# Ring depths of four, four and three in a routed expert stage, with the result store issued by ScalarE

## The reference

```
x = x + 0.5 * experts(layernorm(x))        # 8 experts, top 2, hidden width 256
x = x + attention(layernorm(x))            # 16 heads of 8, softmax, per batch
x = x + 0.5 * experts(layernorm(x))        # the same weights again
x = x + 0.5 * fp4_ffn(layernorm(x))        # weights and activations rounded to FP4 in blocks of 16
x = x + retention(layernorm(x))            # 16 heads, decay, group norm
x = x + 0.5 * fp4_ffn(layernorm(x))
```

## Time and profile before

| | us |
|---|---|
| median of 2 runs (2268.72 and 2268.86) | 2268.79 |
| profiled execution, its own time | 2260.8 |
| its span, first to last instruction | 2259.0 |
| TensorE busy in the span (matmul) | 1542.7 (68%) |
| VectorE, ScalarE, GpSimd busy | 1171.3, 940.7, 557.6 |
| TensorE's mean granted clock | 0.815 of full |

### The profile page before, as it was taken

The page is one execution under the profiler, slowest core; times in us unless marked ns, Lnnn a source line. Parts: engine busy times, 40 slices in busy tenths (PEclk is TensorE's granted clock), DMA queues, the critical chain, the costliest instruction groups (busy, mean ns, idle before and its releaser), DMA issues.

```text
span 2259.0 us, 25733 instructions
## 1 busy us (share of the span) xinstructions
PE 1542.7 (68%) x9017; PEld 837.3 (37%) x9017; DVE 1171.3 (52%) x1765; ACT 940.7 (42%) x1957; POOL 557.6 (25%) x966
## 2 busy tenths in 40 slices
PE   4345454555559999999999853454545467899777
PEld 3234343443111111111111232343434345666566
DVE  5200001111959999999999352111011139968896
ACT  1111111112158888888888721111111134566464
POOL 5720022125440000000000247100222026444411
PEclk9866666777569999999999975666666677999898
DMA  5221222222110101101001022212222210000001
GB/s 188 89 77 58 70 75 81 71 82 91 56 61 18 32 21 32 32 18 44 21 23 32 8 73 89 79 59 70 73 80 70 70 49 19 1 2 2 2 1 38
DMA packets 97457, 116.23 MB, mean 51 GB/s; under 512 B 14368, under 2 KB 76512, under 8 KB 97104
## 3 DMA queue, kind: packets, MB, share of 16 engines
q1 hardware_dynamic: 89136, 97.78, 14.6%
q0 software_dynamic: 8192, 16.79, 2.4%
HBM read 82.28 MB, written 35.26 MB: 52 GB/s over the span
## 4 chain that ended last, share of the span: by engine, by line
PE 52%; DMA 12%; DVE 11%; issue 7%; POOL 6%; ACT 6%; SPq 5%; POOLq 0%; ACTq 0%; DVEq 0%
PE PS L569 13%; DMA slots_in<-slots_x 11%; PE PS L1030 11%; PE PS L1018 8%; PE PS L581 4%; PE PS L1007 4%; DVE neg_half L1165 3%; PE PS L558 3%; ACT probs L1106 2%; POOL slots_x L472 2%; SPq L512 2%; PE PS L1715 2%; SPq L514 2%; ACT slots_out L636 2%; SPq L531 1%
## 5 line engine op out<-in xcount | busy, mean ns | idle before, releaser
L1165 DVE TENSOR_REDUCE neg_half<-PS 128x2 f32<-128x1024 f32 x512 | 601.4, 1220 | 73.2 <-PE PS L1007 58.1
L1106 ACT ACTIVATE probs<-PS 128x512 f32<-128x512 f32 x1024 | 528.8, 603 | 110.8 <-PE PS L1018 109.8
L711 DVE TENSOR_TENSOR shared<-shared,PS 128x512 f32<-128x512 f32 x92 | 63.3, 688 | 830.8 <-PE PS L569 740.4
L558 PE MATMUL PS<-ident,slots_in 128*128 128x128 f32 x184 | 61.4, 436 | 466.9 <-DMA slots_in<-slots_x 444.4
L569 PE MATMUL PS<-slotsT,w_ring 128*128 128x256 f32 x736 | 322.2, 616 | 0.0
L1018 PE MATMUL PS<-qk_all 51*128 51x512 bf16 x1024 | 278.5, 386 | 23.6 <-ACT probs L1106 17.9
L1030 PE MATMUL PS<-probs,Vg 128*32 128x512 f32 x2048 | 273.6, 606 | 0.1
L569 PEld LDWEIGHTS PS<-slotsT,w_ring 128*128 128x128 f32 x736 | 228.9, 326 | 47.5
L623 ACT ACTIVATE slotsT<-PS 128x256 f32<-128x256 f32 x92 | 35.3, 384 | 495.3 <-PE PS L558 471.8
L487 POOL DMA_INDIRECT came<-slots_y,place x128 | 127.9, 999 | 460.6 <-DMA slots_y<-slots_out 423.1
L1007 PE MATMUL PS<-qk_all 48*128 48x512 bf16 x1024 | 199.4, 400 | 42.6 <-DVE neg_half L1165 25.5
(11 more groups left out here) (217 smaller groups left out, 1949.2 us busy)
## 6 DMA issues: line engine op xcount, KB each, us to landing
w_ring<-in_w_experts SPq DMA_DIRECT2D x92, 384.0 KB, 3.1
slots_in<-slots_x SPq DMA_DIRECT2D x92, 128.0 KB, 3.0
slots_y<-slots_out SPq DMA_DIRECT2D x92, 128.0 KB, 1.8
split<-qk_all SPq DMA_DIRECT2D x16, 384.0 KB, 3.3
qk_all<-split SPq DMA_DIRECT2D x64, 96.0 KB
qk_all<-split SPq DMA_DIRECT2D x64, 64.0 KB
slots_x<-tokens_all,place POOLq DMA_INDIRECT x128, 2.2
came<-slots_y,place POOLq DMA_INDIRECT x128, 2.6
```

Of the source, the lines that this page charges most:

```text
L558: last = pe.transpose(bank(0)[:, j * P:(j + 1) * P], slots_in[:, k % RING_TILES, j, :], ident[:, :])
L1106: act.activation(probs[:, n % 2, STRIPS * strip + pair, :], bank(RING_AT + use % RING), ACT.Exp, scale=ATT_SCALE).then_inc(s["exped"], 1)
L1165: dve.tensor_reduce(neg_half[m % 2][:, i % 2, :, at], bank(use_bank(i, m), 2).rearrange("p (s w) -> p s w", s=STRIPS), AX.X, ALU.max, nega ...
```

## The change

The single length `RING_TILES = 3` becomes three lengths: four places for weights, four for rows, three for results. The loads of SP run further ahead: weights three tiles, rows four tiles, and in a turn the rows come before the weights. The store of a tile's results leaves SP and goes to ScalarE's queue: in turn i ScalarE issues, after `result(i)`, the store of tile i - 1, and the last tile's store after the loop. The waits of the loads keep their meaning (a place must be free before it is filled), with the new lengths.

```
-RING_TILES = 3
+W_RING, IN_RING, OUT_RING = 4, 4, 3
...
         def moe_load_weights(sp, n, i):
             k = tile_of(n, i)
-            part, r = i // PART_TILES, k % RING_TILES
+            part, r = i // PART_TILES, k % W_RING
...
-            wait(sp, moe["y_ps"], k - RING_TILES + 1)
+            wait(sp, moe["y_ps"], k - W_RING + 1)
...
         def moe_load_slots(sp, n, i):
...
-            wait(sp, moe["in_ps"], k - RING_TILES + 1)
+            wait(sp, moe["in_ps"], k - IN_RING + 1)
...
-        def moe_store_slots(sp, n, i):
+        def moe_store_slots(act, n, i):
             k = tile_of(n, i)
-            part, r = i // PART_TILES, k % RING_TILES
-            sp.wait_ge(moe["y"], k + 1)
+            part, r = i // PART_TILES, k % OUT_RING
+            act.wait_ge(moe["y"], k + 1)
             at = i % PART_TILES * SLOTS_TILE
-            sp.dma_start(slots_y[part][at:at + SLOTS_TILE, :].rearrange("(j p) c -> p j c", p=P),
+            act.dma_start(slots_y[part][at:at + SLOTS_TILE, :].rearrange("(j p) c -> p j c", p=P),
...
         def moe_sp(sp, n, at_tile=None, between=None):
-            AHEAD = RING_TILES - 1
-            for i in range(AHEAD):
+            for i in range(W_RING - 1):
                 moe_load_weights(sp, n, i)
             if between is not None:
                 between()
-            for i in range(AHEAD):
+            for i in range(IN_RING):
                 moe_load_slots(sp, n, i)
             for i in range(STAGE_TILES):
-                if i + AHEAD < STAGE_TILES:
-                    moe_load_weights(sp, n, i + AHEAD)
-                    moe_load_slots(sp, n, i + AHEAD)
-                moe_store_slots(sp, n, i)
+                if i + IN_RING < STAGE_TILES:
+                    moe_load_slots(sp, n, i + IN_RING)
+                if i + W_RING - 1 < STAGE_TILES:
+                    moe_load_weights(sp, n, i + W_RING - 1)
...
             def result(i):
                 k = tile_of(n, i)
                 act.wait_ge(s["y_ps"], k + 1)
-                wait(act, s[f"out{k % RING_TILES}"], 16 * (k // RING_TILES))
+                wait(act, s[f"out{k % OUT_RING}"], 16 * (k // OUT_RING))
...
                 result(i)
+                if i > 0:
+                    moe_store_slots(act, n, i - 1)
                 if n == 0:
                     prep_act_at(act, i - PART_TILES)
+            moe_store_slots(act, n, STAGE_TILES - 1)
```

More of the change, by code:

```diff
@@ L106, in macaron @@
         rank = sb("rank", [P, TILES, EXPERTS])
-        w_ring = sb("w_ring", [P, RING_TILES, EXPERT_WORDS])
-        slots_in = sb("slots_in", [P, RING_TILES, SLOTS_TILE // P, C])
+        w_ring = sb("w_ring", [P, W_RING, EXPERT_WORDS])
+        slots_in = sb("slots_in", [P, IN_RING, SLOTS_TILE // P, C])
         slotsT = sb("slotsT", [P, 2, SLOTS_TILE])
-        slots_out = sb("slots_out", [P, RING_TILES, SLOTS_TILE])
+        slots_out = sb("slots_out", [P, OUT_RING, SLOTS_TILE])
         came = sb("came", [P, 2, GT, 2, C])
@@ L233, in macaron @@
         moe = stage_sems(ctx, nc, "moe", "xn xT_ps xT logit_ps logits shifted exped weighed members counts experts place scattered0 scattered1 "
-                         "w0 w1 w2 in0 in1 in2 out0 out1 out2 in_ps inT gu silu0 silu h y_ps y came0 came1 half_added x_acc")
+                         "w0 w1 w2 w3 in0 in1 in2 in3 out0 out1 out2 in_ps inT gu silu0 silu h y_ps y came0 came1 half_added x_acc")
         att = stage_sems(ctx, nc, "att", "xn xT_ps xTf q_ps k_ps qkf_half v_ps v_raw qkf rest1 part2 parts V to_dram0 to_dram1 strips filled read neg_step "
@@ L339, in uses_of @@
         def uses_of(k, slot):
-            return (k - slot + RING_TILES - 1) // RING_TILES
+            return (k - slot + OUT_RING - 1) // OUT_RING
         def moe_tokens(dve, n, g):
@@ L481, in moe_gather @@
                 end = tile_of(n, (part + 1) * PART_TILES)
-                for r in range(RING_TILES):
+                for r in range(OUT_RING):
                     pool.wait_ge(moe[f"out{r}"], 16 * uses_of(end, r))
@@ L517, in moe_load_slots @@
             k = tile_of(n, i)
-            part, r = i // PART_TILES, k % RING_TILES
+            part, r = i // PART_TILES, k % IN_RING
             if i % PART_TILES == 0:
                 sp.wait_ge(moe[f"scattered{part}"], SCATTERED * (n // 2 + 1))
-            wait(sp, moe["in_ps"], k - RING_TILES + 1)
+            wait(sp, moe["in_ps"], k - IN_RING + 1)
             at = i % PART_TILES * SLOTS_TILE
@@ L554, in turned @@
                 k = tile_of(n, i)
-                pe.wait_ge(s[f"in{k % RING_TILES}"], 16 * (k // RING_TILES + 1))
+                pe.wait_ge(s[f"in{k % IN_RING}"], 16 * (k // IN_RING + 1))
                 wait(pe, s["inT"], k)
                 for j in range(SLOTS_TILE // P):
-                    last = pe.transpose(bank(0)[:, j * P:(j + 1) * P], slots_in[:, k % RING_TILES, j, :], ident[:, :])
+                    last = pe.transpose(bank(0)[:, j * P:(j + 1) * P], slots_in[:, k % IN_RING, j, :], ident[:, :])
                 last.then_inc(s["in_ps"], 1)
@@ L562, in gate_up @@
                 k = tile_of(n, i)
-                w = w_ring[:, k % RING_TILES, :]
+                w = w_ring[:, k % W_RING, :]
                 pe.wait_ge(s["inT"], k + 1)
-                pe.wait_ge(s[f"w{k % RING_TILES}"], 16 * (k // RING_TILES + 1))
+                pe.wait_ge(s[f"w{k % W_RING}"], 16 * (k // W_RING + 1))
                 wait(pe, s["h"], k - 1)
@@ L634, in result @@
                 act.wait_ge(s["y_ps"], k + 1)
-                wait(act, s[f"out{k % RING_TILES}"], 16 * (k // RING_TILES))
-                act.activation(slots_out[:, k % RING_TILES, :], bank(1)[:, 0:SLOTS_TILE], ACT.Copy
+                wait(act, s[f"out{k % OUT_RING}"], 16 * (k // OUT_RING))
+                act.activation(slots_out[:, k % OUT_RING, :], bank(1)[:, 0:SLOTS_TILE], ACT.Copy
                                ).then_inc(s["y"], 1)
```

1 line of the change is left out of this document (removed).

## The result

The changed kernel took **1663.62 us** (median of 1663.51 and 1663.72) against 2268.79: a ratio of 0.733 [0.730, 0.736], 605 us less. The forecast was 1680, within 1640 to 1800. The profiled execution's span fell from 2259.0 to 1661.6 us, the mean granted clock rose from 0.815 to 0.914.

A forecast was written before the change was run, and what follows sets the result against it. The prediction took the tile loop's circle of result, store and loads as the bound. Savings of 155 + 155 + 149 + 130 = 589 us from 2260.8 leave 1672; with 8.0 for the median, 1680 us, range 1640 to 1800.

The forecast's parts named there:

- What bounds the kernel now: Tile loop: a circle through result, store and loads; transposes stand 444 us for rows, and TensorE resumes at 1.2 GHz.
- The turn that is left: Tile loop: if nothing waits, TensorE sets the turn at 2.8 us, taken as 2.9 for hand-overs.
- ScalarE's issue: Store issue on ScalarE: taken as 0.36 us, between nothing and 3.61; up to about 1.4 lies beside TensorE's work.
- The transfers: Tile loads and stores: 226 GB/s leaves room; 5 us added in each stage for scatter and the clock's rise.
- Stage 2's second part: From the gather's start to the last `down`: 215.4 us falls to 66, with 6 allowed for additions; 149 saved.
- Stage 0's second part: First gather to attention's first scores: tiles outrun GpSimd, ScalarE stands some 15 us; 237.5 falls to 107, 130 saved.
- The other stages only start earlier: Outside the forecast's four stretches in stages 0 and 2: no change in length, only an earlier start.
- loads set the turn: Rival, chance 0.13: weights and rows land one after the other; turn 3.3 or 4.7 us, time 1715 to 1845.
- The clock stays low: Rival, chance 0.07: hand-overs of single banks keep TensorE at 1.2 GHz; turn 5.6 us, time 1930.
- ScalarE's issue is dear: Rival, chance 0.05: the store's issue takes 3.61 us, ScalarE's turn is 5.0, time 1875.
- slower: Rival, chance 0.02: the issue holds ScalarE until earlier transfers are through; at 10 us an issue, time 2390.
- the change doesn't do what it says: Rival, chance 0.03: something else holds the turn as long; only the store's issue is saved, 33 us, time 2236.

The follow-up runs named there:

- run 3: Ten unused matmuls of constants added after `down` in 69 of the 92 turns of the kernel before, keeping TensorE at work: 2141.57 us.
- run 2: The kernel before, with rings of three and SP's old order of loads; only the store moves to ScalarE's queue, a tile later: 2111.23 us.
- Runs 1: The changed kernel with the store back on SP behind the turn's loads, keeping the longer rings and SP's new order: 1685.25 us.
- run 5: The changed kernel with three places for weights instead of four, loaded two tiles ahead: 1689.48 us.
- run 6: The changed kernel with three places for rows instead of four: 1665.31 us.
- run 4: The changed kernel with GpSimd's gathers, bias, layer-norm steps and attention preparation reordered in stage 0's second part: 1643.91 us.

## Why the prediction was right

**What bounds the kernel now** held: the circle through result, store and loads was the turn, and the stand for the rows went from 444 to 20 us. That the wait costs twice held too, by run 3, though run 2 has turns in which the clock stays at 1.00 after a stand. Runs 1 and 2 sharpen it. The circle could be opened at either link, but not equally: the moved store alone takes 157 us, the longer rings with SP's new order 583, both 605. The prediction named the store's place in the order as the reason why the ring didn't help; the place of the loads in time, how many tiles ahead of use they are, was the larger part.

Runs 2 and 5 say which loads. Both have the moved store, and both have three places for weights and load them two tiles ahead, as the kernel before does. They differ in the rows alone: two tiles ahead and behind the weights in run 2, four tiles ahead and in front of them in run 5. That is 2111.23 against 1689.48, 422 us. The fourth place for weights is worth only the other 26, and the fourth place for rows nothing beside it (run 6). So it is the rows' earlier issue that pays. Whether SP's new order would do with three places of each, or four places with the old order, was not run.

**The turn that is left**, 2.8 from the earlier trace rows, taken as 2.9, is 2.84. The reading of that one undisturbed turn carried the forecast. **ScalarE's issue**, taken at 0.36 between nothing and 3.61, shows 0.37 and lies beside TensorE's work. The far end was put down to busy queues, but in the trace of the kernel before the issues that follow it on SP, from 8.49 on, take 0.43 to 0.59 us while the transfers run at 489 GB/s; so busy transfers alone don't make an issue that long.

**The transfers** held, with the allowance too large. In the first parts 24 turns of 2.84 are 68.2, and store, landing and GpSimd's start 3.9: that is 72.1. The prediction had 2.7 for the tail (the median landing of the store has risen since, from 1.8 to 3.6) and 5 for scatter and clock, which is nearly all unneeded: the windows show 1.00 and 0.99.

**Stage 2's second part**: 61.0 against 66. The 6 us for the additions were too many; TensorE's whole wait for `hidden`, over all 92 turns, is 4.8 us in the row of L580 above.

**Stage 0's second part**: 109.7 against 107, with stands of 11.00, 10.12 and 1.55 us where I had some 15, 9 and 3. The sum is right within 3 us, and run 4, which takes most of the two long stands away, gains 20 us by GpSimd's order alone.

**"The other stages only start earlier"** is the step that failed, by 7.4 us between attention's first scores and stage 2's first free turn. Some 6 of these lie in attention's last turns, where the clock fell; the last section has the rows. What made it fall was not tested.

**The sum**: 589 forecast, 597 measured. Half of the forecast's excess of 16 us is this; the other 8 was the distance of the median from the profiled execution of the kernel before, which the changed kernel doesn't have (both its runs lie within 0.2 us). That the total comes so near is partly luck: the allowances were about 5 us too large in each of three stretches, and attention's 7.4 took back half of that.

**Slips in the working**, none of which moves the forecast: in the rival of late loads, (9.3 + 0.4) / 2 is 4.85 us and not 4.7, so its upper end is near 1860 and not 1845; SP's own work adds up to 1.53 us and not 1.6; and of TensorE has 178 records in 200 to 300 us, so the ten are turns and not instructions.

**The two rules of the Trainium skill.** By the Trainium skill, "DMA: Bandwidth & Descriptors" (section "Issuing engines are not separate DMA queues"), the moved store would be worth its issuing time. Runs 1 and 2 measure it: 157 us with the old loads and 22 with the new ones, against the 33 that 92 issues of 0.36 make. The 22 are within the rule, the 157 are not: with the old loads the move also frees the order of SP's queue. How the transfers of two issuing engines share the engines below them, no run here shows.

By the Trainium skill, "TensorE: Matmul & The Clock Gate" (section "A second HAM failure mode: psum-queue depth-cycling"), the hand-overs of single banks could have kept the clock swinging. The trace doesn't show that here: with bank 0 and bank 1 handed over in every turn, TensorE's granted clock is 1.00 from 92 to 160 us. TensorE has no idle time there, so the idle times that the rule speaks of don't arise; in run 5 they do, and the clock is 1.00 too.

**The rivals**: *loads set the turn* didn't come true, but one place is all that lay between. With three places for weights (run 5) `gate_up` does wait, and the turn is 3.22, near the lower of that rival's two turns. *The clock stays low*, *ScalarE's issue is dear*, *slower* and *the change doesn't do what it says* are refuted by the rows of the turn and by the time.

## What to carry to other kernels

When a transfer is waited for, follow it back through its queue: a load that stands behind a store that waits for a result closes a circle, and in this kernel the length of that circle was the turn. Let no load whose place is free stand behind a wait, and issue each load at least its landing time ahead of use, before moving stores between engines (here 583 us against 157); then look for the one turn in the trace that ran without a wait, since it tells the turn that will be left. And read the queue of an experiment as closely as that of the kernel, because a doubled transfer with one place to land in measures its own wait.

## What I had not expected

**Landing under load.** The store's median time from issue to landing doubled, from 1.8 to 3.6 us, and the weights' rose from 3.1 to 3.7. The page's rows, first of the kernel before, then of the changed one:

```profile
slots_y<-slots_out SPq DMA_DIRECT2D x92, 128.0 KB, 1.8
```
```profile
w_ring<-in_w_experts SPq DMA_DIRECT2D x92, 384.0 KB, 3.7
slots_y<-slots_out ACTq DMA_DIRECT2D x92, 128.0 KB, 3.6
```

**The clock at attention's end.** The last turns of attention are the same code in both kernels. Windows from near the last turns to attention's end, first of the kernel before, then of the changed one:

```profile
1295.00:1318.00 23.00, 17.82 (x122) 6.96 (x120) 12.88 (x40) 14.08 (x28) 6.93 (x21) 1.00 0.02 4
```
```profile
1008.00:1037.00 29.00, 24.43 (x120) 8.59 (x120) 14.69 (x46) 14.27 (x28) 6.95 (x21) 0.71 0.01 3
```

ScalarE does the same 28 instructions in 23 us there and in 29 here, with TensorE's granted clock at 1.00 and at 0.71. Just before, the clock was 1.00 in both, with TensorE busy 90% of the time (85.51 of 95 us and 86.52 of 96). Why it falls in the one and not in the other stays open.

It isn't a matter of this one pair of traces. The stretch from attention's first scores to stage 2's first free turn is 830.5 us in the kernel before and 830.8 in run 3, which keeps the old rings and loads; in the changed kernel and the nine other runs it is 837.9 to 841.1. But each kernel was traced once, and the traced execution of the kernel before is 8.0 us shorter than the median. So the 7.4 here and those 8.0 may be one and the same drop, missing by chance from the traced execution; no second trace of the kernel before shows whether that is so.
